# Reordered step lists and a last pass divided between VectorE and GpSimd, in an adaLN block with a routed mixture of experts

## What is computed

```
mod = (silu(c) @ wmod).reshape(2, 6, 1, 256)      # sa, ca, ga, sb, cb, gb
h = layernorm(x) * (1 + ca) + sa
x = x + ga * attn_block(h)       # gated linear recurrence over the tokens, output
                                 # projection, then: h + (silu(h2 @ Wgate) * (h2 @ Wval)) @ Wout
h = layernorm(x) * (1 + cb) + sb
scores = softmax(h @ gate_weight.T);  top 4 of 16 experts per token
y = sum over the 4 experts of  w_e * (silu(g) * u) @ down_e.T     # FFN 176 wide
y = y + shared expert (352 wide)
out = x + gb * y                 # gb per channel, at least 0.25 in size
```

## Time and profile before

| what | value |
|---|---|
| median of 3 runs | 368.24 us (368.22 to 368.97) |
| profiled execution, its own time | 365.12 us |
| span of that execution (first to last instruction) | 363.3 us |
| TensorE busy | 317.4 us, 87% |
| VectorE busy | 209.1 us, 58% |
| ScalarE busy | 176.0 us, 48% |
| GpSimd busy | 162.8 us, 45% |

### The profile page before, as it was taken

One profiled execution on the slowest core, in us unless ns is written; L12 is line 12 of the kernel. 1 busy time (PEld: TensorE's weight loads), 2 busy tenths in 40 slices (PEclk: granted clock), 3 DMA queues, 4 the chain that ended last, 5 costly groups with the idle time before them and its releaser, 6 DMA issues.

```text
span 363.3 us, 5639 instructions
## 1 busy us (share of the span) xinstructions
PE 317.4 (87%) x1424; PEld 236.1 (65%) x1424; DVE 209.1 (58%) x607; ACT 176.0 (48%) x338; POOL 162.8 (45%) x156
## 2 busy tenths in 40 slices
PE   6998989999999997999699787999999999999500
PEld 3785555766678876877497565777777777777300
DVE  4778998589576546594558834344343343343146
ACT  3488986798883533553271212443443444444200
POOL 3364487910001003256355571466566566666510
PEclk9889999999999999999988989999999999999855
DMA  6911031100019772002899464577766767765483
GB/s 206 359 68 59 1 115 59 60 0 0 2 48 361 158 144 73 2 17 98 231 321 325 150 204 157 111 111 108 121 113 105 115 118 109 120 113 62 56 231 133
DMA packets 43993, 44.91 MB, mean 124 GB/s; under 512 B 3387, under 2 KB 39995, under 8 KB 43963
## 3 DMA queue, kind: packets, MB, share of 16 engines
q1 hardware_dynamic: 35659, 33.66, 32.5%
q0 software_dynamic: 8304, 10.88, 18.7%
HBM read 27.74 MB, written 16.79 MB: 123 GB/s over the span
## 4 chain that ended last, share of the span: by engine, by line
PE 67%; DVE 15%; ACT 5%; DMA 5%; issue 4%; POOL 1%; SPq 1%; DVEq 0%; ACTq 0%; POOLq 0%
PE ps L1773 15%; PE ps L1800 10%; PE ps L1599 3%; PE ps L1361 3%; PE ps L1604 3%; PE ps L1600 3%; PE ps L1378 3%; PE ps L1362 3%; PE ps L1759 3%; PE ps L1786 3%; DMA acc_rows<-w,ids 2%; PE ps L1411 2%; PE ps L1418 1%; DVE w L1341 1%; DMA w<-in_wmod 1%
## 5 line engine op out<-in xcount | busy, mean ns | idle before, releaser
L546 POOL DMA_INDIRECT acc_rows<-w,ids x47 | 73.4, 1562 | 52.2 <-ACT w L866 49.6
L1773 PE MATMUL ps<-wup,w 128*128 x188 | 63.6, 460 | 1.5 <-DVE hm L1287 1.4
L1313 DVE TENSOR_TENSOR sg<-sg,ps 128x176 f32<-128x176 f32 x47 | 15.9, 338 | 68.4 <-ACT sg L858 68.4
L1800 PE MATMUL ps<-wdown,w 88*128 x188 | 48.6, 380 | 0.6 <-DVE w L1321 0.6
L533 POOL DMA_INDIRECT xs_rows<-h3x,slots x32 | 33.3, 1040 | 20.9 <-issue 20.9
L866 ACT ACTIVATE w<-ps,wv 128x256 f32<-128x256 f32 x47 | 22.3, 475 | 36.7 <-PE ps L1800 35.9
L1773 PEld LDWEIGHTS ps<-wup,w 128*128 128x128 f32 x188 | 32.0, 190 | 12.0 <-issue 1.9
L441 POOL TENSOR_TENSOR wsm_lo<-w,wsm_hi 128x512 fp32r<-128x512 f32 (+1 forms) x9 | 13.7, 1534 | 53.9 <-ACT wsm_hi L803 35.5
L1800 PEld LDWEIGHTS ps<-wdown,w 88*128 88x128 f32 x188 | 31.9, 190 | 3.8 <-issue 1.3
L858 ACT ACTIVATE sg<-ps 128x176 f32<-128x176 f32 x47 | 14.9, 317 | 33.3 <-PE ps L1773 33.3
L1599 PE MATMUL ps<-b_hi,wff_hi 128*128 128x512 f32 x64 | 26.9, 420 | 2.1 <-ACT w L756 1.3
(11 more groups left out here) (290 smaller groups left out, 705.9 us busy)
## 6 DMA issues: line engine op xcount, KB each, us to landing
xt<-xs_rows SPq DMA_DIRECT2D x47, 144.0 KB, 2.2
wup<-in_wmoe SPq DMA_DIRECT2D x4, 1408.0 KB
wdown<-in_wmoe SPq DMA_DIRECT2D x1, 2816.0 KB
xs_rows<-mod SPq DMA_DIRECT2D x17, 144.0 KB, 2.2
acc_rows<-mod SPq DMA_DIRECT2D x2, 1152.0 KB, 9.2
wdown<-in_wff SPq DMA_DIRECT2D x4, 512.0 KB, 6.4
w<-acc_rows SPq DMA_DIRECT2D x8, 256.0 KB, 4.6
w<-in_wsm SPq DMA_DIRECT2D x3, 512.0 KB, 9.2
```

Of the source, the lines that this page charges most:

```text
L546: nc.gpsimd.indirect_dma_start(acc_rows[n][:, :], bass.IndirectOffsetOnAxis(ids[:, i:i + 1], 0), ysb[i % YBUF], None, compute_op=ALU.add). ...
L1773: last = mm(bank(1, i)[:, 0:2 * FE].rearrange("p (w n) -> p w n", w=2), xT[i % 2][:, k * P:(k + 1) * P], up[:, k, :, bass.ds(e, FE)], star ...
L1800: last = mm(bank(3, i)[:, 0:C], hT[i % 2][:, h * P:(h + 1) * P], down[:, bass.ds(e + h * C, C)], start=h == 0, stop=h == 1)
```

## The change

1. TensorE: `up.1.3` is taken apart into its gate (`ug.1.3`) and its value half (`uv.1.3`), with `logits.0` and `tx.0` between them, and `rank.0` comes ahead of `down.1.2` and `up.1.4`. `tm` waits for both halves of `acc` at its start.
2. ScalarE: `ehigh.0`, `ehigh.1` and `ehigh.2` come earlier; `exp.0` comes ahead of `hid.1.3`; `h3hi.0` comes later. Of `acc.1`, the second half goes to VectorE.
3. VectorE: `lgsub.0`, `topk.0` and `rank.0` come around one `prod` earlier, `h3lo.0` and `pre.1` later, `egated.0.0` ahead of `hn3.1`. `early` is taken apart: `ends` stays in its place, the rest goes behind `elo.0.2`. `need` goes behind `elo.1.1`. `late` leaves the list: its four parts run in the first four steps of the tile loop.
4. GpSimd: `elow.1` comes ahead of `root.0.1`; `root.1.1` comes one `scatter` later.
5. SP: the register loads ahead of the small transfers that empty the lists' ends are made four at a time.
6. End: GpSimd does the multiplications and additions of sequence 1, VectorE those of sequence 0; the write-outs alternate.

```diff
 TENSOR_PLAN
-    down.0.4 t2.1 up.0.7 down.0.5 up.1.0 down.0.6 down.0.7 up.1.1 tm.0 rows up.1.2 down.1.0 down.1.1 t3.0 up.1.3
-    logits.0 tx.0 down.1.2 up.1.4 rank.0 down.1.3 up.1.5 down.1.4 up.1.6 down.1.5 up.1.7 down.1.6 down.1.7 eg.0.0 tm.1
+    down.0.4 t2.1 up.0.7 down.0.5 up.1.0 down.0.6 down.0.7 up.1.1 tm.0 rows up.1.2 down.1.0 down.1.1 t3.0 ug.1.3
+    logits.0 tx.0 uv.1.3 rank.0 down.1.2 up.1.4 down.1.3 up.1.5 down.1.4 up.1.6 down.1.5 up.1.7 down.1.6 down.1.7 eg.0.0 tm.1
 SCALAR_PLAN
-    silu.0.5 silu.0.6 hid.0.5 hid.0.6 h2hi.1.0 h2hi.1.1 silu.0.7 h2.1.0 h2.1.1 silu.1.0 hid.0.7 hid.1.0 acc.0 rows
-    silu.1.1 hid.1.1 ehigh.0 silu.1.2 hid.1.2 h3.0 silu.1.3 ehigh.1 tx.0 hid.1.3 silu.1.4 exp.0 h3hi.0 hid.1.4 ehigh.2
-    silu.1.5 hid.1.5 silu.1.6 hid.1.6 silu.1.7 hid.1.7 acc.1 esilu.0.0 esilu.0.1 h3.1 ehid.0.0 h3hi.1 exp.1 tx.1
+    silu.0.5 silu.0.6 hid.0.5 ehigh.0 hid.0.6 h2hi.1.0 h2hi.1.1 silu.0.7 h2.1.0 h2.1.1 ehigh.1 silu.1.0 hid.0.7 hid.1.0
+    acc.0 rows silu.1.1 hid.1.1 ehigh.2 silu.1.2 hid.1.2 h3.0 silu.1.3 tx.0 exp.0 hid.1.3 silu.1.4 hid.1.4
+    silu.1.5 hid.1.5 h3hi.0 silu.1.6 hid.1.6 silu.1.7 hid.1.7 acc.1 esilu.0.0 esilu.0.1 h3.1 ehid.0.0 h3hi.1 exp.1 tx.1
 VECTOR_PLAN
-    hn3.0 prod.1.2 h3.0 hidlo.1.2 prod.1.3 lgsub.0 hidlo.1.3 prod.1.4 topk.0 rank.0 h3lo.0 hidlo.1.4 pre.1
-    prod.1.5 hidlo.1.5 prod.1.6 hidlo.1.6 prod.1.7 hidlo.1.7 sum3.1 var3.1 hn3.1 egated.0.0 h3.1 egated.0.1
-    lgsub.1 elo.0.0 topk.1 rank.1 early elo.0.1 egated.0.2 h3lo.1 elo.0.2 need egated.1.0
-    late elo.1.0 egated.1.1 sum.0 finish.0 elo.1.1 egated.1.2 elo.1.2 sum.1 finish.1
+    hn3.0 prod.1.2 h3.0 hidlo.1.2 lgsub.0 prod.1.3 topk.0 rank.0 hidlo.1.3 prod.1.4 hidlo.1.4 pre.1
+    prod.1.5 hidlo.1.5 h3lo.0 prod.1.6 hidlo.1.6 prod.1.7 hidlo.1.7 acc.1 sum3.1 var3.1 egated.0.0 hn3.1 h3.1 egated.0.1
+    lgsub.1 elo.0.0 topk.1 rank.1 ends elo.0.1 egated.0.2 h3lo.1 elo.0.2 early egated.1.0
+    elo.1.0 egated.1.1 sum.0 finish.0 elo.1.1 need egated.1.2 elo.1.2 sum.1 finish.1
 POOL_PLAN
-    root.0.0 root.1.0 elow.0 root.0.1 elow.1 elow.2 scatter.0.0 scatter.0.1 root.1.1 scatter.0.2 scatter.0.3 scatter.1.0 ...
+    root.0.0 root.1.0 elow.0 elow.1 root.0.1 elow.2 scatter.0.0 scatter.0.1 scatter.0.2 root.1.1 scatter.0.3 scatter.1.0 ...
...
-            for b in range(NB):
-                for h in range(2):
-                    sp.wait_ge(s("y_ready"), 2 * b + h + 1)
+            for h in range(2):
+                for b in range(NB):
+                    sp.wait_ge(s("y_pool" if b else "y_ready"), h + 1)
...
+            for k in range(NACC):
+                for h in range(2):
+                    given = tok(W[1][k])[:, 2 * h:2 * h + 2, :]
+                    rows = hm[1][:, 2 * h:2 * h + 2, :]
+                    pool.wait_ge(*acc_in[(k * NB + 1) * 2 + h])
+                    link(nc.gpsimd.tensor_tensor(given, given, gbr[:, 1, :].unsqueeze(1).broadcast_to([P, 2, C]), ALU.mult))
+                    last = nc.gpsimd.tensor_tensor(rows, rows, given, ALU.add)
...
+                nc.vector.tensor_scalar(W[b][3][:, 1, :], PB(b)[:, 1, :], gbc[:, KC + 1, b:b + 1], None,
+                                        ALU.mult).then_inc(s("wo_sb"), 1)
...
+            late_table = [late_reached, late_stepped, late_offsets, lambda: to_registers(EARLY, NTILE)]
...
+                if step < len(late_table):
+                    late_table[step]()
...
             for k in range(NACC):
-                for b in range(NB):
+                for b in range(1):
```

More of the change, by code:

```diff
@@ L100 @@
     sqq.0 chunkhi.3 chunkhi.4 chunk.3 wsm.6 chunk.4 sqv.1 chunkhi.5 chunk.5 sqq.1 sqk.1
-    root.0.0 root.1.0 elow.0 root.0.1 elow.1 elow.2 scatter.0.0 scatter.0.1 root.1.1 scatter.0.2 scatter.0.3 scatter.1.0 scatter.1.1 scatter.1.2 scatter.1.3
+    root.0.0 root.1.0 elow.0 elow.1 root.0.1 elow.2 scatter.0.0 scatter.0.1 scatter.0.2 root.1.1 scatter.0.3 scatter.1.0 scatter.1.1 scatter.1.2 scatter.1.3
 """
@@ L380, in _, with empty_ends @@
             sp.wait_ge(s("tab_ready"), 1)
-            def empty_end(e):
-                row = nc.sync.value_load(ends[0:1, e:e + 1], min_val=1 + SPACE * e, max_val=1 + SPACE * e + CAP)
-                sp.dma_start(xs_rows[bass.ds(row, P), :], empty_rows).then_inc(s("emptied"), 16)
+            def empty_ends(lo, hi):
+                rows = [nc.sync.value_load(ends[0:1, e:e + 1], min_val=1 + SPACE * e, max_val=1 + SPACE * e + CAP)
+                        for e in range(lo, hi)]
+                for row in rows:
+                    sp.dma_start(xs_rows[bass.ds(row, P), :], empty_rows).then_inc(s("emptied"), 16)
             def load_tile(i):
@@ L392, in load_tile @@
                 sp.dma_start(xt[:, i % RING, :], xs_rows[bass.ds(row, P), :]).then_inc(xt_in[i % RING], 16)
-            for e in range(NE // 2):
-                empty_end(e)
+            for e in range(0, NE // 2, 4):
+                empty_ends(e, e + 4)
             sp.wait_ge(s("tab_ready"), 2)
@@ L399, in _ @@
                 load_tile(i)
-            for e in range(NE // 2, NE):
-                empty_end(e)
+            for e in range(NE // 2, NE, 4):
+                empty_ends(e, e + 4)
             for i in range(RING, EARLY):
@@ L561, in _ @@
                 add_rows(i)
+            pool.wait_ge(s("rows_sb"), 1)
+            pool.wait_ge(s("tw_used"), 3 * NB)
+            for k in range(NACC):
[5 more added lines that the diff above has]
+                    last = nc.gpsimd.tensor_tensor(rows, rows, given, ALU.add)
+                    if k:
+                        last.then_inc(s("y_pool"), 1)
+                    else:
+                        link(last)
         @block.scalar
@@ L768, in acc @@
                 act.wait_ge(s("modc_ready"), 2)
-                for c in range(KC):
+                for c in range(KC - b):
                     nc.scalar.activation(W[b][3][:, c, :], PB(b)[:, c, :], ACT.Copy,
@@ L1241, in early_table @@
                 link(nc.vector.tensor_tensor_scan(full_incl, one_row, full_tiles, 0.0, ALU.mult, ALU.add))
-                assign(0, EARLY, full_incl, full_step)
+                reached(0, EARLY, full_incl)
+                stepped(0, EARLY, full_step)
+                offsets(0, EARLY)
                 to_registers(0, EARLY)
@@ L1293, in _ @@
                 "o1": o1, "osig": osig, "sqe": sqe, "gated": gated, "outlo": outlo, "wo": wo, "var2": var2, "hn2": hn2, "h2lo": h2lo,
-                "prod": prod, "hidlo": hidlo, "pre": pre, "sum3": sum3, "var3": var3, "h3": h3, "hn3": hn3, "h3lo": h3lo, "lgsub": lgsub, "topk": topk,
-                "egated": moe_gated, "elo": moe_lo, "rank": rank, "early": early_table, "need": late_need_, "late": late_table, "sum": sum_out, "finish": finish,
+                "prod": prod, "hidlo": hidlo, "acc": acc, "pre": pre, "sum3": sum3, "var3": var3, "h3": h3, "hn3": hn3, "h3lo": h3lo, "lgsub": lgsub, "topk": topk,
+                "egated": moe_gated, "elo": moe_lo, "rank": rank, "ends": ends_, "early": early_table, "need": late_need_, "sum": sum_out, "finish": finish,
             }
@@ L1739, in _ @@
                 "ig": ig, "iglo": iglo, "ga": ga, "ssk": ssk, "og": og, "ssv": ssv, "u": u, "mem": mem, "oc": oc, "vo": vo, "wo": wo, "tw": tw, "t2": t2,
-                "up": ff_up, "down": ff_down, "tm": tm, "t3": t3, "logits": logits, "rank": rank, "rows": rows, "tx": tx, "st": sum_to_tokens,
+                "up": ff_up, "ug": ff_gate, "uv": ff_value, "down": ff_down, "tm": tm, "t3": t3, "logits": logits, "rank": rank, "rows": rows, "tx": tx, "st": sum_to_tokens,
                 "eg": moe_gate, "ev": moe_value, "edown": moe_down,
```

54 lines of the change are left out of this document (35 added, 19 removed).

## The result

The changed kernel took 375.46 us (median of four, 374.34 to 376.30), the kernel before beside it 368.61 us: ratio 1.0222, 95% interval 1.0176 to 1.0269. Ratios with an interval are of the fast runs of either kernel, those within 1.5% of its fastest, so they are not the quotients of the medians beside them. The forecast was 367.2, 1.05 us faster than before. Measured again on two other chips, the same two kernels stood at 0.9967 (0.9925 to 1.0008) and 1.0077 (1.0023 to 1.0130). So two questions have to be answered: what the change costs wherever it runs, and what came on top in the first measurement.

A forecast was written before the change was run, and what follows sets the result against it. The prediction took TensorE (67% of the chain) as the bound, with VectorE behind its last product. Terms -3.5 -1.0 +1.6 +1.85 = -1.05 gave span 362.25, time 364.1; the median's 3.1 above made 367.2 us, range 365.4 to 369.5.

The forecast's parts named there:

- I take 1.06, by type and operation: At the end: each GpSimd pass of 128x512 was priced at 1.06 us, near the 1.04 row of a multiplication.
- the other splits meet no such pass: GpSimd's `elow.0` and `elow.2` were to meet no VectorE pass with two SBUF inputs, so no cost was added.
- Part 1, the late table: Ahead of the loop, at `st.0`: `late` leaving VectorE's list starts the second half 2.1 us earlier, full clock gives 1.4: -3.5.
- the products that use it start over 1 us behind it: Loop steps 0 to 3: copies delayed about 0.9 us by `late`'s parts were to be covered, costing nothing.
- Part 2, `elow.2` and the `prod` order: Near 158 to 164 us: moving the split and `pre.1` removes TensorE's 0.86 idle and small gaps: -1.0 us.
- Part 2, `elow.1`: Near 125.5 us: the moved GpSimd split holds up `pre.0` and so `down.0.7`: +1.6 us.
- rival 2: Clock falls behind the new gap at 129.6 us, getting back costs 1.4: 368.6 us, no difference; chance 0.12.
- the forecast's rule: When VectorE and GpSimd passes both read SBUF, VectorE with two inputs there, the second waits for the first's end.
- Part 3, the small edits: `acc.1` on two engines, `egated.0.0`, earlier scatters and tile loads (4 us), register loads, `root.1.1`: in all about 0.
- Part 4, the end: Passes divided between GpSimd and VectorE take turns at 1.51 us a pair, GpSimd last: +1.85 us.
- The bound from the subtraction: At the end: if a GpSimd pass takes 1.30 us, like the subtraction row, the end comes 3.7 us later.
- rival 1: At the end: a GpSimd pass costs 1.30 us or more, +1.9: 369.1 us, slower; decides from 1.28; chance 0.15.

The follow-up runs named there:

- k8: k7 with the whole table (early, need, late) back in VectorE's list as before the change, none of it in the loop: 363.57 us, ratio 0.9848 to the kernel before.
- k7: Changed kernel with all 16 end passes on VectorE and ScalarE's and GpSimd's second and third split steps moved so that they run after `hn3.0`: 365.46 us.
- a3: The changed kernel, unaltered, profiled a third time, beside b2 on the same chip: ratio 1.0077 to the kernel before.
- k9: k7 with the first of the four late parts behind `egated.1.2` in VectorE's list, three left in the loop: 364.26 us, ratio 0.9843 to the kernel before.
- b2: The kernel before, unaltered, profiled a third time, beside a3 on the same chip: 365.28 us.
- b3: The kernel before, unaltered, profiled a fourth time, beside a4 on the same chip: median 366.58 us.
- after_again: The changed kernel, unaltered, measured again on another chip: 368.38 us, ratio 0.9967 to the kernel before.
- k5: k2 with SP's first four tile loads waiting for ScalarE's last `hid` of the shared expert: 374.64 us, ratio 1.0294 to the kernel before.
- k6: k2 with SP's register loads one at a time, as before the change: 364.16 us, ratio 1.0001 to the kernel before.
- k2: Changed kernel with all 16 end passes back on VectorE: 370.0 us, ratio 1.0046 to the kernel before.
- a4: The changed kernel, unaltered, profiled once more beside b3 on the same chip: median 367.12 us.
- k1: The kernel before with only the changed end, its passes divided between GpSimd and VectorE: 371.9 us, ratio 1.0063 to the kernel before.
- k4: The kernel before with only the late table moved, its four parts in loop steps 0 to 3: 369.64 us, ratio 0.9958 to the kernel before.
- k3: Changed kernel with the three `ehigh` and three `elow` steps back where the kernel before has them: 374.79 us, ratio 1.0144 to the kernel before.

## Why the prediction was wrong

The forecast was a span of 362.25 and a time of 367.2; the profile has 372.9, the median is 375.46. Two steps of it failed wherever the kernel ran: the price of a GpSimd pass ("I take 1.06, by type and operation"), which was 1.25, and "the other splits meet no such pass", where `elow.2` met `hn3.0` for 1.48 us. On top came the stall, which had no term.

**Part 1, the late table, -3.5: the mechanism right, the size -3.5 to -5.6.** k8 against k7 gives 2.0 for the wait and 1.5 behind it, by the working that was forecast. The loop was costed at nothing, 0.3 if short; it gives 0.75 back. The step "the products that use it start over 1 us behind it" doesn't hold in the first tiles: in k7, a3 and the first measurement TensorE has 0.4 to 0.5 us idle ahead of the first down products, and in k9, with one part less in the loop, it hasn't. The clock's share, 1.4 in the forecast, is 1.7 where the half clock lasts 3.4 us and 3.4 where it lasts 6.8, as in b2 and b3.

**Part 2, `elow.2` and the `prod` order, -1.0: right, -1.2 to -1.3.** The wait of 0.86 at 163.91 is gone.

**Part 2, `elow.1`, +1.6: right, +1.63.** The clock stayed at full there, so rival 2 didn't happen at its place.

**Part 2, "the other splits meet no such pass": wrong, +1.48.** Two things were missed. `elow.2` and `hn3.0` both follow the end of `root.0.1`, so they start together by construction. And the forecast's rule is for VectorE passes with two inputs in SBUF; `hn3.0` has one tensor input there, and the trace shows it held up for 1.48 us. With `elow.2` moved behind it, in k7, it takes 1.38 again. The Trainium skill (SBUF — State Buffer, Who interferes with whom) lists tensor_scalar among the operations that can take the shared port pair; the forecast had its eye on passes with two SBUF inputs, the same section's other case. The trace agrees with the section at 143.75, where 1.38 became 2.86. Behind that wait the clock fell in the first profile (1.7 us), in after_again, in k5 and in k6, and not in k2, a3 and a4.

**Part 3, the small edits, 0: nothing speaks against it.** TensorE waits 3.34 at `t3.1`, where it waited 3.36. The tile loads come 1.6 us earlier and not 4 (145.3 us behind the product near 64 in a3, 146.8 before), and nothing waited for them.

**Part 4, the end, +1.85: the mechanism right, the size wrong, +3.3.** The step that failed is "I take 1.06, by type and operation". A GpSimd pass of 128x512 with two different inputs took 1.25, whether it multiplies by a broadcast row or adds; the row at 1.04 multiplies a tile by itself. With 1.25 the forecast's own working gives 3.4. The bound from the subtraction (3.7) was the nearer one, and rival 1 comes nearest to what happened, though 1.25 lies below the 1.28 that it names. A pair took 1.67 where 1.51 was forecast. The 3.3 is in five of the six profiles with the divided end; in a3, where GpSimd's first pass came later, it is 3.7.

**The sum.** -3.5 -1.3 +1.6 +1.5 +0.75 +3.3 = +2.3 us where -1.05 stood: 1.45 of the difference is the end's price, 1.5 the second split, 0.75 the loop, less 0.3. Without the 1.5 that part 1 gains by the clock it is +3.8; the weighted spans, with the 1.65 that they leave out, give 4.2 and 2.7 on two chips, and 5.6 on a third from few runs. With part 1 at -5.6, as between b2 and a3, the sum is +0.25. So without the stall the change costs 0.25 to 2.3 us by these terms. The ratio of 0.9967 in after_again lies next to the forecast's 0.9972 by luck: the kernel before had the lower granted clock there, 0.943 on average against 0.948.

**What no term had: the stall.** In the first measurement's profile it cost 5.0 (a wait of 3.70 where 0.78 stood, and half clock behind it). With the clock at 147 (1.7) and the loop's 1.94 instead of 0.75 that makes 10.2, less 0.58 of the start and 0.3 of the first landing: the 9.6 between the two profiles, within 0.3. The forecast then added 3.1 to get from the profiled execution to the median, as before; the measured step is 0.8. That took 2.3 off the miss, which is 8.3 in the medians. Stretched loads are in five profiles, after and k1 to k4, and in none of fourteen others. k1 to k4 ran on one chip and thirteen of the others on three more (the first measurement's chip isn't recorded), so it goes with the chip as far as these runs can tell; what causes it there is open. The kernel before was never profiled with it; on the chip of k1 to k4 its weighted span was 347.5, against 344.8 to 346.3 on the three others. k1, which has its lists up to the end, shows that stretched loads can go by without a cost, k4 that they can cost as much in an order that is before's but for the late table. That the changed kernel suffered more because it had removed that very wait is likely, and only argued.

## What to carry to other kernels

Before a step is moved ahead on one engine, look at what waits for the event that it now follows: two steps released by one signal start together, and if the two engines can hold each other up, one of them pays in full. Price a pass on another engine by a row with the same number of different inputs, not by the same operation's name. A wait that is removed gives back its length and also the half clock behind it, and here that second part was 1.7 us in some executions and 3.4 in others. So compare kernels by span times granted clock as well as by time, and profile each more than once before a difference of a few us is explained.

## What the runs showed of the hardware

- The granted clock fell to half (1.2 GHz) behind TensorE's wait of 3.3 us or more at `t3.1` in 17 of 19 profiles, behind the one of 3.1 at `st.0` in six of six, behind 2.67 at `t3.0` in four of seven, and right behind the ones of 1.07 to 1.19 at the same places in none. How long it stayed there behind the same wait differed from 3 to 14 us between runs of one kernel: up to 5 us of time.
- Four normalising instructions of 128x256 with one tensor input in SBUF and two per-row scalars took 2.86 us beside a GpSimd pass and 1.38 without.
- When VectorE and GpSimd both queue passes with two SBUF inputs, they alternate, in all six profiles of the divided end: 1.59 each on GpSimd, 1.63 to 1.74 on VectorE, against 1.25 and 0.69 alone. A pair costs 1.67, while VectorE alone does two passes in 1.34.
- In three of the four profiles of one chip (k2, k3, k4), and in the first of the changed kernel, ScalarE or VectorE (in k3 both) went on about 4 to 6 us after the work that it waited for had ended, beside tile loads of SP that took 7.1 to 7.9 us for four instead of 3.6 to 3.9. GpSimd's issuing went on every 1.27 us in the same stretch. Fourteen profiles, thirteen of them on three other chips, have neither.
